# First cross-attention of a decoder: TensorE's slots ordered by kind of product, and the queries' products in the keys' PSUM bank

## The reference

```python
def _L0_xattn_ref(inputs_q, inputs_kv, Wq, bq, Wk, bk, Wv, bv, Wo, bo):
    q = jnp.einsum('bqm,mhd->bqhd', inputs_q, Wq) + bq
    k = jnp.einsum('bkm,mhd->bkhd', inputs_kv, Wk) + bk
    v = jnp.einsum('bkm,mhd->bkhd', inputs_kv, Wv) + bv
    q = q / jnp.sqrt(jnp.asarray(HD, q.dtype))
    attn = jnp.einsum('bqhd,bkhd->bhqk', q, k)
    attn = jax.nn.softmax(attn, axis=-1)
    out = jnp.einsum('bhqk,bkhd->bqhd', attn, v)
    return jnp.einsum('bqhd,hdm->bqm', out, Wo) + bo
```

## Time and profile before

| | us |
|---|---|
| median of 3 runs | 1551.73 (1549.59 to 1555.68) |
| the profiled execution | 1551.16 |
| its span in the profile | 1549.3 |
| TensorE busy (84% of the span) | 1294.3 |
| TensorE weight loads (71%) | 1097.0 |
| VectorE busy (66%) | 1028.1 |
| ScalarE busy (48%) | 740.8 |
| GpSimd busy (15%) | 226.8 |

### The profile page before, as it was taken

One profiled execution on the slowest core, in us unless ns is written; L12 is line 12 of the kernel. 1 busy time (PEld: TensorE's weight loads), 2 busy tenths in 40 slices (PEclk: granted clock), 3 DMA queues, 4 the chain that ended last, 5 costly groups with the idle time before them and its releaser, 6 DMA issues.

```text
span 1549.3 us, 27234 instructions
## 1 busy us (share of the span) xinstructions
PE 1294.3 (84%) x9826; PEld 1097.0 (71%) x9826; DVE 1028.1 (66%) x2389; ACT 740.8 (48%) x1801; POOL 226.8 (15%) x235
## 2 busy tenths in 40 slices
PE   4889798976999999999999999954478886969409
PEld 3879787876888888888888888743356664759409
DVE  5875575544666666666666666668857776885974
ACT  4442324234655555565555655531055553335563
POOL 4334252524000000000000000000133332000100
PEclk9999898987999999999999999976589998989759
DMA  8100101030000000000000000020100000300001
GB/s 268 35 15 4 38 1 41 0 129 20 10 11 11 10 10 10 10 10 10 10 10 10 10 10 0 1 58 27 53 1 2 2 2 27 107 27 1 0 0 43
DMA packets 34520, 40.43 MB, mean 26 GB/s; under 512 B 4889, under 2 KB 29066, under 8 KB 34442
## 3 DMA queue, kind: packets, MB, share of 16 engines
q1 hardware_dynamic: 33614, 39.24, 8.3%
q10 hardware_dynamic: 828, 0.14, 0.1%
HBM read 35.36 MB, written 4.01 MB: 25 GB/s over the span
## 4 chain that ended last, share of the span: by engine, by line
PE 57%; DVE 14%; issue 4%; ACT 4%; DVEq 0%; POOL 0%; ACTq 0%; POOLq 0%
PE bank L718 10%; PE bank L719 8%; PE bank L720 8%; PE bank L925 5%; PE bank L909 5%; PE bank L917 4%; PE bank L885 4%; DVE amax L2233 2%; PE bank L1122 1%; DVE z L1746 1%; PE bank L1132 1%; PE bank L1106 1%; PE bank L871 1%; PE bank L1072 1%; PE bank L1088 1%
## 5 line engine op out<-in xcount | busy, mean ns | idle before, releaser
L1497 ACT ACTIVATE prob<-bank,nmx 100x361 f32<-100x361 f32 x256 | 142.5, 560 | 124.4 <-DVE nmx L2032 123.4
L2032 DVE TENSOR_REDUCE nmx<-bank 100x1 f32<-100x361 f32 x256 | 124.7, 528 | 44.5 <-PE bank L909 33.9
L1988 DVE TENSOR_TENSOR oTl<-bank,oTh 128x100 fp32r<-128x100 f32 x128 | 33.3, 260 | 120.1 <-ACT oTh L1483 120.1
L661 POOL MEMSET v1z<- 100x1024 f32 x1 | 1.0, 951 | 733.0 <-DVE x L2095 733.0
L718 PE MATMUL bank<-cxTh,wxkh 128*128 128x362 f32 x256 | 99.3, 388 | 0.8 <-DVE kTl L1989 0.6
L925 PE MATMUL bank<-pT,vv 128*64 128x100 f32 (+1 forms) x1536 | 95.6, 260 | 0.7 <-DVE oTl L1988 0.7
L2049 DVE TENSOR_SCALAR prob<-prob,rsum 100x361 f32<-100x361 f32 x256 | 92.9, 405 | 4.5
L925 PEld LDWEIGHTS bank<-pT,vv 128*64 128x64 f32 (+1 forms) x1536 | 70.3, 138 | 35.9 <-issue 23.1
L1483 ACT CAST oTh<-bank 128x100 fp32r<-128x100 f32 x128 | 31.7, 248 | 128.6 <-PE bank L925 128.6
L917 PE MATMUL bank<-ident,prob 100*128 100x100 f32 (+1 forms) x768 | 89.6, 253 | 1.9 <-DVE prob L2049 1.9
L917 PEld LDWEIGHTS bank<-ident,prob 100*128 100x128 f32 (+1 forms) x768 | 84.4, 151 | 7.2 <-DVE prob L2049 2.7
(11 more groups left out here) (378 smaller groups left out, 3775.1 us busy)
## 6 DMA issues: line engine op xcount, KB each, us to landing
cx<-in_ctx_dram SPq DMA_DIRECT2D x32, 128.0 KB, 2.0
xc<-in_ctx_dram SPq DMA_DIRECT2D x32, 128.0 KB
parked_weights<-parking SPq DMA_DIRECT2D x9, 256.0 KB, 5.5
mask_i<-in_mask_BxS_ik_dram SPq DMA_DIRECT2D x16, 141.0 KB
w<-in_L_attn_W_dram SPq DMA_DIRECT2D x2, 1024.0 KB, 13.6
cx<-in_ctx_dram SPq DMA_DIRECT2D x16, 105.0 KB, 2.0
xc<-in_ctx_dram SPq DMA_DIRECT2D x16, 105.0 KB
x<-in_x_dram SPq DMA_DIRECT2D x4, 400.0 KB
```

The source lines that it names most:

```text
L1497: nc.scalar.activation(prob[:, h % 4, :], bank[S_BANKS[e]][0:T, 0:S], ACT.Exp, bias=nmx[:, h:h + 1], accum_out=psum_[:, h:h + 1]).then_inc ...
L2032: nc.vector.tensor_reduce(nmx[:, h:h + 1], bank[S_BANKS[e]][0:T, 0:S], AX_X, ALU.max, negate=True).then_inc(xa_max, 1)
```

## The change

In TensorE's slot the split products come first (S, K, V, O), then the plain ones (T, Q, C, W). Value item 1 is computed at pair 2 instead of pair 1. The queries' product goes into the keys' bank instead of the weighted values' bank: it waits for this slot's keys to be out of it (`xa_kl` of pair + 8 + 1), and the next keys wait for the queries to be out (`xa_ql`); W no longer waits for them. ScalarE takes the keys out between the two exponentials and the queries at the end of its slot; VectorE takes the keys out ahead of the reciprocal and the queries at the end. What is computed is the same, with the same instructions.

```diff
--- before.py
+++ after.py
@@ -452,7 +452,7 @@
         LASTP = B * PAIRS0
         S_BANKS, T_BANKS, O_BANK, K_BANK, V_BANK, W_BANK = (0, 1), (2, 3), 4, 5, 6, 7
         K_START, Q_START = (5, 0, 1), (4, 3)
-        V_SLOT = {0: 0, 1: 1, 3: 2, 4: 3, 6: 4, 7: 5}
+        V_SLOT = {0: 0, 2: 1, 3: 2, 4: 3, 6: 4, 7: 5}
 
         def v_item(j):
 
@@ -933,23 +933,32 @@
                 if final:
                     pe.wait_ge(xa_kl, pair + 1)
                 score_pair(p, odd)
-                if odd and not ends:
-                    at_least(pe, xa_ol, pair - 2)
-                    queries(p, 2 * T * i + 2 * T, bank[O_BANK])
                 if not final:
                     if p == 0:
                         pe.wait_ge(xa_cl, KD * b + 2 * KD)
                     pe.wait_ge(xa_kl, pair + PAIRS0)
+                    if p or not odd:
+                        pe.wait_ge(xa_ql, PAIRS0 * i + PAIRS0 + (p if odd else 0))
                     keys(p, 1 - odd, bank[K_BANK])
+                if p in V_SLOT and not (final and p >= 6):
+                    values_slot(b, p, odd)
+                if p == 2 and not (starts and not odd):
+                    pe.wait_ge(xa_ol, pair - 2)
+                    output_product(bank[W_BANK])
                 if not (starts and n < 1):
                     pe.wait_ge(xa_p, 2 * pair)
                     at_least(pe, xa_pT, pair - 1)
                     transposed_pair((p - 1) % PAIRS0)
-                if p == 2 and not (starts and not odd):
-                    pe.wait_ge(xa_ol, pair - 2)
-                    output_product(bank[W_BANK])
-                if p in V_SLOT and p != 1 and not (final and p >= 6):
-                    values_slot(b, p, odd)
+                if odd and not ends:
+                    pe.wait_ge(xa_kl, pair + PAIRS0 + 1)
+                    queries(p, 2 * T * i + 2 * T, bank[K_BANK])
+                if not ends and p in (5, 6):
+                    k = p - 5
+                    if k == 0:
+                        pe.wait_ge(xa_x, b + 1)
+                    else:
+                        pe.wait_ge(xa_cl, KD * b + 2 * KD + 1)
+                    context(b + 2, k, bank[W_BANK])
                 if not (starts and n < 2):
                     if p == 2:
                         pe.wait_ge(xa_va, 3 * b + 2)
@@ -958,18 +967,7 @@
                         pe.wait_ge(xa_vd, 3 * b + 3)
                     pe.wait_ge(xa_pT, pair - 1)
                     at_least(pe, xa_ol, pair - 2)
-                    if odd and not ends:
-                        pe.wait_ge(xa_ql, PAIRS0 * i + PAIRS0 + p + 1)
                     weighted_pair((p - 2) % PAIRS0)
-                if p == 1:
-                    values_slot(b, p, odd)
-                if not ends and p in (5, 6):
-                    k = p - 5
-                    if k == 0:
-                        pe.wait_ge(xa_x, b + 1)
-                    else:
-                        pe.wait_ge(xa_cl, KD * b + 2 * KD + 1)
-                    context(b + 2, k, bank[W_BANK])
 
             def values_slot(b, p, odd):
 
@@ -1509,13 +1507,13 @@
                     context_high(b + 2, p - 6, odd, bank[W_BANK])
                 at_least(act, xa_t, pair - 1)
                 exponent(pair, p, 0)
-                if odd and not ends:
-                    queries_high(PAIRS0 * i + PAIRS0 + p, p, bank[O_BANK])
-                exponent(pair, p, 1)
                 if not final:
                     keys_high(pair + PAIRS0, p, bank[K_BANK])
+                exponent(pair, p, 1)
                 if not (starts and n < 1):
                     probabilities(pair - 1, (p - 1) % PAIRS0)
+                if odd and not ends:
+                    queries_high(PAIRS0 * i + PAIRS0 + p, p, bank[K_BANK])
 
             for k, o in enumerate((W_BANK, T_BANKS[0])):
                 context_high(0, k, 0, bank[o])
@@ -2039,16 +2037,16 @@
                     context_low(b + 2, p - 6, odd, bank[W_BANK])
                 if p == 3 and not (starts and not odd):
                     added(b - 1)
-                if odd and not ends:
-                    queries_low(PAIRS0 * i + PAIRS0 + p, p, bank[O_BANK])
+                if not final:
+                    keys_low(pair + PAIRS0, p, bank[K_BANK])
                 dve.wait_ge(xa_exp, 2 * pair + 2)
                 nc.vector.reciprocal(rsum[:, 2 * p:2 * p + 2], psum_[:, 2 * p:2 * p + 2]).then_inc(xa_r, 1)
                 dve.wait_ge(xa_r, pair + 1)
                 for e in range(2):
                     h = 2 * p + e
                     nc.vector.tensor_scalar(prob[:, h % 4, :], prob[:, h % 4, :], rsum[:, h:h + 1], None, ALU.mult).then_inc(xa_p, 1)
-                if not final:
-                    keys_low(pair + PAIRS0, p, bank[K_BANK])
+                if odd and not ends:
+                    queries_low(PAIRS0 * i + PAIRS0 + p, p, bank[K_BANK])
 
             dve.wait_ge(xa_zero, 2)
             for n, (low, raw, high) in enumerate(((wxkl, wxk, wxkh), (wxvl, wxv, wxvh))):
```

## The result

The changed kernel takes 1578.39 us (median of 4 runs, 1575.09 to 1579.41) against 1551.97 us of before (4 runs, 1549.59 to 1555.68): a ratio of 1.0164, 95% interval 1.0139 to 1.0190, slower by 26.4 us. The forecast was 1575.5.

A forecast was written before the change was run, and what follows sets the result against it. TensorE was taken to bound the pair loop. Even batches +0.65 and odd +2.34 us gave 17.9 over six turns; with first and last turns 23.9 in all, 1575.5 us forecast, range 1560 to 1593.

The forecast's parts named there:

- Value bank at pairs 0 and 3: Value product directly behind keys waits for VectorE's copy of the previous item: +0.51 and +0.67 us even, +0.50 and +0.61 odd.
- Key bank, odd batches: Queries wait until their slot's keys are copied out, to +3.25 us: pairs 1 and 2 +0.77, pair 5 +0.90.
- Second exponential: On ScalarE behind the keys' copy, it ends 0.55 us later; only even pair 1 meets it, at 3.15 us.
- Price of a kind: Changing between split and plain fp32 products costs TensorE almost nothing; entering and leaving partial-array products costs about 0.10 to 0.16 us.
- V behind K: Value product directly behind the key product in TensorE's slot: nothing extra taken, bound 0.15 us a slot.
- C ahead of W: Context transposes moved ahead of the weighted values at pairs 5 and 6: -0.14 us, bounds 0 and -0.2.
- Queries behind T: Query product moved from behind scores to behind transposes costs 0.63 us instead of 0.69: -0.06, bounds +0.1 and -0.15.
- Queries before the next keys: Next keys need the queries copied out of the shared bank: 0.3 us of cover by estimate, costed at nothing.
- The rule weighed: Weight loads pulled ahead across bank waits would restart stalls about 0.1 us sooner, giving 1571; the prediction rejected this.
- Boundaries worth 0.15 or more: Rival: fewer plain-to-split changes on TensorE make the change win from 0.15 us each; 1536 at 0.25; chance 0.09.
- Late queries: Rival: VectorE's late copy of the queries' low half holds the next keys; +20 us, 1595; chance 0.10.
- Half waits: Rival: copies move forward, so bank waits are 2.6 instead of 5.2 us per two batches; 1555; chance 0.07.

The follow-up runs named there:

- the version that keeps the savings: Queries back, with value item 1 at pair 1 behind the keys and transposes ahead of values at pair 0 of even batches and the last; 1543.54 us.
- item 1 back: Changed kernel with value item 1 computed at pair 1 again, behind the keys, instead of pair 2; 1560.20 us, ratio 1.0055.
- queries back: Changed kernel with queries behind the scores in the weighted values' bank again, ScalarE's and VectorE's order as before, item 1 still at pair 2; 1563.36 us.
- the last kernel above: The version that keeps the savings, with VectorE's value copy ahead of the maxima at pair 0 replacing most early transposes there; 1538.03 us, ratio 0.9927.

## Why the prediction was right, step by step

- **What bounds it.** Right. Of the 28.4 us by which the loop is longer, 27 are new idle time of TensorE. The chain of before was not TensorE alone over the whole loop, as I had it: 0.9% of it are ScalarE's exponentials and about 1% VectorE's maxima and scaled probabilities. That changes no term.
- **Value bank at pairs 0 and 3.** Right in place, cause and size: +0.52 and +0.71 (even), +0.61 and +0.71 (odd) against +0.51, +0.67, +0.50, +0.61. Moving the copy alone takes it away.
- **Key bank, odd batches.** Right in place and nearly in size: pairs 1 and 2 grow by 0.82 and pair 5 by 0.83 (forecast 0.77 and 0.90), released by the keys' low half at 716.46 - 713.26 = +3.20 of the slot (forecast +3.25).
- **Second exponential.** Right: even pair 1 is 3.13 (forecast 3.15).
- **Price of a kind.** Right, and now measured: 0.027 us there and back, against 0.32 for the shape. Nearly all of the long first distance behind a plain product (0.07 us of keys, with them split in two) comes back in the plain product ahead of it (0.06 us of transposes).
- **V behind K.** Right at the value taken: no extra, 0.23 from the first matmul. The 0.04 a slot that I had V and T save together are 0.00 at pair 4 of even batches and 0.03 at pair 7.
- **C ahead of W.** Right: even pair 5 is -0.16 against -0.14, pair 6, with the 0.04 of V, -0.17 against -0.18.
- **Queries behind T.** The one term mis-sized. I had T 0.47 + Q 0.78 = 1.25; the medians of the loop are T 0.53 + Q 0.80 = 1.33. The 0.47 was T's length in front of a value product; in front of Q it is 0.53. So Q costs 0.71 over T alone (0.62), where it cost 0.69 before, and the saving of 0.06 isn't there. The odd batch is 0.47 us over my count (0.09 to 0.11 at pairs 0, 3, 4, 6 and 7, 0.05 at 1 and 2, and 0.07 under at 5) and the even batch, which has no queries, 0.08. So most of the 0.56 us by which a turn is longer than forecast, some 0.4, is this term.
- **Queries before the next keys.** Right to cost nothing: no keys wait for the queries' low half in the loop's list of waits. Behind pair 4 of an odd batch it ends at 713.16 + 0.42 = 713.58, and the next keys start at 713.91, 0.3 us of cover as in my estimate.
- **The sum.** Loop +28.4 against +23.9. First turn 3.4 (2.5), six turns 21.3 (17.9), last 3.8 (3.5). So the loop grew by 4.5 us more than forecast, and the median came out 2.9 us from the number (1578.4 against 1575.5) and not further because the time outside the loop was shorter: 4.5 us in the profiled execution, 2 by the medians. That part is luck.
- **The rule weighed.** The load started with its matmul at 716.46 after 0.92 us of idle. A query product behind such a wait took 0.87 in front of W at pair 1, where one that did not wait took 0.80, and the value product behind its wait 1.47 (649.66 - 648.19) to 1.50 against 1.40: each stall cost 0.07 to 0.10 us more to restart, near the 0.1 that I had counted. The page's rule that weight loads are pulled ahead (the Trainium skill, TensorE: Matmul & The Clock Gate, Part 3, The mechanism) did not reach across the new waits; if it had, the turn would have been some 0.5 us shorter.
- **The rivals.** Boundaries worth 0.15 or more: refuted by the keys split in two, 1553.5 where 0.15 us each gives 1569, and by the version that keeps the savings, 1543.5 where it gives 1531. Late queries: did not come. Half waits: did not come; the copy stayed at +2.35.

## What to carry to other kernels

Before grouping work by kind, price the change of kind by adding changes, not by reading the first distance behind one: here it was 0.03 us, while in and out of a product of 64 columns was 0.32. On an engine that is busy 99% of a stage, the work between two uses of one bank is what hides the copy out of it; a move that brings the uses together makes the engine wait for what is left of the copy, 0.5 to 0.8 us here, against the 0.04 to 0.2 that it saves at a boundary. And look on the other engine first: one copy placed ahead of two maxima gave back 20 of the 26 us that the new order had lost.

## What the runs showed that I had not expected

- A 1.7 us wait of TensorE at pair 0 of the last odd batch was followed by 3.4 us at the lower of its two clock levels in two kernels (item 1 back, queries back; the 0.58 above is a mean over a window), and the slot took 6.74 us. With item 1 back:

```profile
1002.00:1005.40 3.40, 3.40 (x19) 2.62 (x19) 0.55 (x2) 0.53 (x2) 0.00 (x0) 0.50 0.00 0
```

In the changed kernel the same wait passed at full clock, and so did one of 0.6 and one of 1.7 us behind it:

```profile
1015.40:1020.50 5.10, 3.43 (x34) 2.49 (x32) 2.73 (x7) 2.05 (x8) 0.00 (x0) 1.00 0.01 2
1020.50:1034.00 13.50, 11.26 (x106) 9.19 (x102) 7.47 (x21) 6.51 (x22) 0.00 (x0) 1.00 0.00 1
```

So such a wait costs 1.6 us more in some executions; these runs don't show what decides it.
- The time outside the loop, where all ten kernels have the same code but for the end of the last slot, ranges from 926.6 us (the last kernel above, mean granted clock 0.926) to 936.2 (queries back, 0.919) in their profiles, with before at 934.6 and after at 930.1. It goes with the granted clock. So medians of a few executions can be some us off what an edit did, and the loop's length, from its first to its last score product, is the better measure.
- Six transposes are 0.62 us long in front of the weighted values, 0.53 in front of a query or context product and 0.47 in front of a value or output product, counted from start to start: how long a phase looks depends on what comes behind it, so only whole slots compare.
